# Cross-attention on one core: the first memory block loaded early, and a new order of transfers at the entry into the attention

## What is computed

```python
memory_proj = einsum('bme,de->bmd', memory, W_mem)
scores = einsum('bnd,bmd->bnm', hidden_states, memory_proj) / sqrt(D)
attn = softmax(scores)
memory_context = einsum('bnm,bmd->bnd', attn, memory_proj)
gate = sigmoid(concatenate([hidden_states, memory_context]) @ W_gate.T + b_gate)
fused = hidden_states + gate * memory_context
out = rmsnorm(fused) * norm_w
```

## Time and profile before

| | |
|---|---|
| median of 3 runs | 1613.51 us (1610.14 to 1613.7) |
| the profiled execution's own time | 1613.78 us |
| its span (first to last instruction) | 1612.0 us |
| mean granted TensorE clock | 0.995 of full |
| PE busy | 1578.6 us, 98% of the span |
| DVE busy | 1035.4 us, 64% |
| ACT busy | 458.2 us, 28% |
| DMA | mean 158 GB/s |

### The profile page before, as it was taken

One profiled execution on the slowest core, in us unless ns is written; L12 is line 12 of the kernel. 1 busy time (PEld: TensorE's weight loads), 2 busy tenths in 40 slices (PEclk: granted clock), 3 DMA queues, 4 the chain that ended last, 5 costly groups with the idle time before them and its releaser, 6 DMA issues.

```text
span 1612.0 us, 21593 instructions
## 1 busy us (share of the span) xinstructions
PE 1578.6 (98%) x6912; PEld 1302.4 (81%) x6912; DVE 1035.4 (64%) x1437; ACT 458.2 (28%) x767; POOL 17.9 (1%) x37
## 2 busy tenths in 40 slices
PE   7999999999999889999999999999999999999998
PEld 5888888888888768888888877887888888888886
DVE  5664668777777654576456744666545677777766
ACT  4333342222222332244223432253224211111111
POOL 0000000000000000000000000000000000000000
PEclk9999999999999999999999999999999999999999
DMA  9997533333334848566575748467555544444452
GB/s 200 237 225 172 137 105 118 104 116 114 113 118 122 190 125 200 146 173 178 157 176 143 201 145 198 132 166 186 152 177 148 177 164 168 169 173 158 169 182 98
DMA packets 211618, 255.22 MB, mean 158 GB/s; under 512 B 19840, under 2 KB 136576, under 8 KB 211328
## 3 DMA queue, kind: packets, MB, share of 16 engines
q1 hardware_dynamic: 211584, 254.87, 56.9%
HBM read 166.72 MB, written 85.98 MB: 157 GB/s over the span
## 4 chain that ended last, share of the span: by engine, by line
issue 99%; POOLq 0%; POOL 0%; DVE 0%; DVEq 0%
POOL rstd L585 0%; POOLq L583 0%; DVE region_f L1257 0%; POOLq L585 0%; DVEq L49 0%; POOL minus_half L581 0%; POOLq L1456 0%
## 5 line engine op out<-in xcount | busy, mean ns | idle before, releaser
L1283 PE MATMUL bank<-region_t,region_l 128*128 128x512 f32 x3072 | 704.5, 390 | 7.3 <-DVE region_l L266 5.2
L1283 PEld LDWEIGHTS bank<-region_t,region_l 128*128 128x128 f32 x3072 | 576.9, 188 | 130.3 <-issue 10.6
L1283 PE MATMUL bank<-region_n,region_l 128*128 128x512 f32 x1536 | 356.4, 391 | 5.9 <-DVE region_l L266 5.9
L1283 PEld LDWEIGHTS bank<-region_n,region_l 128*128 128x128 f32 x1536 | 290.3, 189 | 67.0 <-DVE region_l L266 6.4
L1283 PE MATMUL bank<-region_t,region_n 128*128 128x512 f32 x960 | 220.7, 392 | 10.8 <-DVE region_t L266 10.8
L1283 PEld LDWEIGHTS bank<-region_t,region_n 128*128 128x128 f32 x960 | 181.8, 190 | 49.2 <-DVE region_t L266 11.2
L723 ACT CAST region_l<-bank 128x512 fp32r<-128x512 f32 x128 | 75.0, 586 | 344.9 <-DVE bank L1066 344.7
L1066 DVE STREAM_TRANSPOSE bank<-region_f 128x512 f32<-128x512 f32 x128 | 88.7, 716 | 128.0 <-DMA region_f<-prob_scratch 125.8
L266 DVE TENSOR_TENSOR region_t<-region_f,region_t 128x1024 fp32r<-128x1024 f32 (+2 forms) x70 | 102.1, 1492 | 67.6 <-ACT region_t L597 60.5
L1324 PE MATMUL bank<-region_t,region_l 128*128 128x512 f32 x576 | 135.8, 389 | 0.0
L1324 PEld LDWEIGHTS bank<-region_t,region_l 128*128 128x128 f32 x576 | 108.1, 188 | 22.5
(11 more groups left out here) (58 smaller groups left out, 882.6 us busy)
## 6 DMA issues: line engine op xcount, KB each, us to landing
region_f<-in_ctx SPq DMA_DIRECT2D x128, 256.0 KB, 5.8
prob_scratch<-prob SPq DMA_DIRECT2D x128, 256.0 KB, 2.7
region_f<-prob_scratch SPq DMA_DIRECT2D x128, 256.0 KB, 4.5
region_f<-in_x SPq DMA_DIRECT2D x64, 256.0 KB, 6.1
region_f<-in_x SPq DMA_DIRECT2D x128, 128.0 KB, 2.7
region_f<-zx_scratch SPq DMA_DIRECT2D x32, 512.0 KB, 3.4
region_f<-in_x SPq DMA_DIRECT2D x32, 512.0 KB, 3.2
out<-region_f SPq DMA_DIRECT2D x31, 512.0 KB, 2.8
```

What stands on the lines that cost most here:

```text
L1283: mm = nc.tensor.matmul(dst, lhs(a), rhs(b), start=first and n == 0, stop=last and n == len(PASSES) - 1)
```

## The change

The raw mt block 0 gets tiles 8 and 9 and is loaded some 260 us earlier, right behind the loads of z pair 2. Its transposes go to tiles 0 and 1 (they were 8 and 9), one product earlier in pair 14. Blocks 1 to 3 are then loaded in the order of use, 1, 2, 3, where it was 3, 1, 2. Of the mn loads, block 1 comes as soon as mt halves 0 to 3 are split, block 0 still ahead of the exchange of unit 0, and block 2 goes behind that exchange, where only block 3 stood.

```diff
-        MT0_SLOT = (0, 1, 2, 0)
-        MT0_TF = [f_tile[k] for k in (8, 9, 8, 9, 2, 3, 4, 5)]
+        mt0_raw = [F[:, 4 * KW * k:4 * KW * (k + 2)] for k in (8, 2, 4, 8)]
+        mt0_tf = [f_tile[k] for k in (0, 1, 0, 1, 2, 3, 4, 5)]
...
+            sp.wait_ge(w7_ready, W7[S1])
+            load_mt(0, 0, mt0_raw[0])
+            with sp.Fori(0, NPAIR - 3) as p:
+                pair_sp(p)
+            pair_sp(NPAIR - 3, loads=False)
...
-            sp.wait_ge(zt_t, 2 * NPAIR)
-            load_mt(0, 0)
             p = NPAIR - 2
             store_zx(p, 0, slice(0, BANK), EV_C11, zx_stored[0])
-            sp.wait_ge(mt_t, HPJ)
-            load_mt(0, 3, MT0_SLOT[3])
-            store_zx(p, 1, slice(0, D), EV_C21, zx_stored[2])
             sp.wait_ge(z_ready, NPROD * NPAIR - 1)
             load_mt(0, 1)
-            store_zx(p, 0, slice(BANK, D), EV_C12, zx_stored[1])
+            store_zx(p, 1, slice(0, D), EV_C21, zx_stored[2])
             sp.wait_ge(z_ready, NPROD * NPAIR)
             load_mt(0, 2)
+            store_zx(p, 0, slice(BANK, D), EV_C12, zx_stored[1])
+            sp.wait_ge(mt_t, HPJ)
+            load_mt(0, 3, mt0_raw[3])
             store_zx(p + 1, 0, slice(0, BANK), EV_C11, zx_stored[0])
+            sp.wait_ge(mt_ready, HPJ * 2)
+            load_mn(0, 1)
             store_zx(p + 1, 1, slice(0, D), EV_C21, zx_stored[2])
+            store_zx(p + 1, 0, slice(BANK, D), EV_C12, zx_stored[1])
...
-            sp.wait_ge(mt_t, MTS)
-            load_mn(0, 1)
-            store_zx(p + 1, 0, slice(BANK, D), EV_C12, zx_stored[1])
-            sp.wait_ge(mt_ready, HPJ * 3)
-            load_mn(0, 2)
             for i in range(3):
                 sp.wait_ge(zx_stored[i], 16 * NPAIR)
             load_mn(0, 0)
             exchange(0, first=True)
+            sp.wait_ge(mt_ready, HPJ * 3)
+            load_mn(0, 2)
             sp.wait_ge(mt_ready, MTS)
             load_mn(0, 3)
...
-                if first and j == 1:
+                if first and j == 0:
+                    dve.wait_ge(zt_t, 2 * NPAIR)
+                elif first and j == 1:
                     dve.wait_ge(mt_ready, h - 1)
...
             def block_first(i):
+                if i == 2:
+                    mt_transpose(0, 0, first=True)
                 if i == 3:
-                    mt_transpose(0, 0, first=True)
-                if i == 4:
                     mt_transpose(0, 1, first=True)
```

More of the change, by code:

```diff
@@ L261, in tf_half @@
         def tf_half(h, first=False):
-            return (MT0_TF if first else b_tf)[h].rearrange("p (t m) -> p t m", t=CT)
+            return (mt0_tf if first else b_tf)[h].rearrange("p (t m) -> p t m", t=CT)
         def minus_hi(dst, src, hi):
@@ L392, in _, with load_mt @@
             load_zraw(2, 1)
[L393 to L398, removed]
+            def load_mt(b, j, dst=None):
+                load_quadrants(sp, b_in[j] if dst is None else dst, mem[b, BANK * j:BANK * (j + 1), :], C, mt_loaded[j])
             def load_mn(b, j):
@@ L1012, in mt_transpose @@
                     dve.wait_ge(mt_t, b * MTS + j * HPJ)
-                rows = b_in[MT0_SLOT[j] if first else j].rearrange("p (b t j) -> p t b j", t=CT, j=SQ)
+                rows = (mt0_raw if first else b_in)[j].rearrange("p (b t j) -> p t b j", t=CT, j=SQ)
                 nb = BANK // SQ // HPJ
```

## The result

| | before | changed |
|---|---|---|
| median of 9 runs | 1613.52 us (1610.14 to 1616.2) | 1608.92 us (1604.82 to 1610.09) |
| profiled span | 1612.0 us | 1607.1 us |
| ratio, 95% interval | | 0.9971 (0.9962 to 0.9979) |

The changed kernel is 4.6 us faster, 0.29%. Forecast were 1607.3 us (1603.5 to 1611.0) and a gain of 6.4 us. The sign is right and the time lies in the range; the median is 1.6 us above the forecast, and the shortfall lies in the second part, as the experiments show. By the prediction's own yardstick, that 4.8 us tell a change from none, these 4.6 us count as "same", which it gave 0.25; the interval of the ratio lies clear of 1 all the same.

What follows compares the result with a forecast made beforehand. PE, 98% busy, bounds the kernel; its entry loses 16.6 us to gaps and slow clock. Scores of unit 2 come 7.2 us earlier (3.9 from mt loads), minus 0.8 slow clock: 6.4 us off, 1607.3 us, range 1603.5 to 1611.0.

Steps and rivals of the forecast that it cites:

- second part: Exchange of unit 0 and mn loads at the entry: transposes 8.1 us earlier, scores of unit 2 at 578.5, not 585.74.
- First part: mt loads: block 1 first removes PE's gap at 527.96 and its slow stretch, 2.17 + 1.7 = 3.9 us.
- The early load costs nothing: Load of mt block 0 at about 241: no cost; without cover at most 4.5 us, once.
- Block 3 last of the mt loads: VectorE's transpose 6: block 3 lands by 534.5, needed at 534.8, 1.7 us slack; 2 us later costs 0.5 to 1.
- The exchange, 561.2: Unit 0's first transposes: first store 549.1 plus 11.0 exchange, 0.3 tail of mn 0, 0.85 for loads behind.
- The chain of 16.4 us: VectorE and ScalarE, transposes to scores of unit 2: not shortened, 16.4 us, so scores at 577.6 at the earliest.
- The landing of mn 3: Last mn load behind the exchange: lands at 568.7, between 566.9 and 570.4; scores of unit 2 9.8 us later.
- Slow clock in the scores of unit 2: PE's scores of unit 2 after small gaps: price 0 or 1.7 us, taken as 0.8.
- B: Second part gives its gain back: mn 3 at 571 or exchange at 564, plus slow clock; gain 3.2, 1610.5; chance 0.20.
- A: mn loads in time, queue behind the exchange costs nothing: scores of unit 2 at 576.5, gain 9.2, 1604.5; chance 0.15.
- Rival C: Loads behind the exchange mix with its last transfer, landing with mn 3 at 569: 1.4 us slower, 1615.2; chance 0.04.
- Rival D: mt block 1 still late, beyond 526; gap at 528 stays in part; gain 3 at most, 1610.8; chance 0.04.

Runs made afterwards that it cites:

- e10: The changed kernel, unaltered, measured and profiled once more: 1609.54 us, ratio 0.9965 against the kernel before.
- e1: Changed kernel with the mt part alone; mn loads and last z store as in the kernel before: 1610.05 us, ratio 0.9974.
- e3: Changed kernel with mt block 0 loaded late again and its transposes at their old places in pair 14: 1609.55 us, ratio 0.9978.
- e4: Changed kernel loading only the first 128 of 512 columns of mn blocks 2 and 3 of batch 0: 1605.73 us, ratio 0.995.
- e7: Changed kernel with mn 2 loaded ahead of mn 0 and so ahead of the exchange: 1607.9 us, ratio 0.9966.
- e5: Changed kernel with mn 3's cast and low part behind the last probability group, low part also behind unit 1's maxima: 1607.44 us, ratio 0.9958.
- e6: Changed kernel with the casts and low parts of mn 2 and mn 3 both moved behind the last probability group: 1606.81 us, ratio 0.996.

## Why the prediction was right, and where it was off

From the scores of unit 0, in us:

| | before | forecast | changed | changed again (e10) |
|---|---|---|---|---|
| first store of probabilities | 13.0 | 13.0 | 13.0 | 13.0 |
| first transposes | 29.3 | 25.1 | 25.7 | 24.5 |
| cast of mn 3 | 33.9 | 32.6 | 34.9 | 34.0 |
| scores of unit 2 (D) | 45.7 | 42.4 | 44.7 | 43.8 |

- **First part, 3.9 us: right.** The gap and its slow stretch are gone, and e1 alone gains 4.2 us by the ratio, 3.9 by the medians. "The early load costs nothing" holds; that it gives a microsecond at most (e3) was not said.
- **Block 3 last of the mt loads: right, with more air than said.** Transpose 6 doesn't wait in the changed kernel; in e3 it does, 0.53 us, and PE takes no harm.
- **The exchange, 561.2: nearly right.** 25.7 and 24.5 us from the scores of unit 0, forecast 25.1. Its tail of 0.85 us "for loads behind" was 1.6 in one profile and 0.4 in the other (end of issues to transposes: 5.3 and 4.1 us against 3.65). That the sum came out is in part luck: this stretch alone scatters by 2.6 us, from 3.3 to 5.9, over the profiles with 2 MB behind it.
- **The chain of 16.4 us, and 9.8 us from mn 3's landing to the scores: exact.** 16.4 in e1, e4 and e7; 9.8 in the changed kernel (571.64 to 581.43) and in e10 (570.55 to 580.34).
- **The landing of mn 3: the term that was mis-sized.** Forecast 568.7 (566.9 to 570.4), which is 32.6 us after the scores of unit 0; measured 34.9 and 34.0. From the first issue the two blocks took 14.4 us in the first profile and 13.6 in the second: at the forecast's upper bound, and beyond it. The rate for the second block was right: it landed 4.5 us after the first in both (567.17 to 571.64, 566.07 to 570.55), as that bound has it. Wrong was the lower bound, 1.8 us of start and 8.3 of data from the issue on, and the middle taken because of it. When SP issued the first block, the exchange's own transfers still stood ahead of it in the queue, and these landed only with the transposes, 5.3 and 4.1 us later. So the landings are better counted from the transposes: the first block 4.7 and 5.1 us behind them, the second 4.5 behind the first, 9.2 and 9.5 us in all. The forecast left 568.7 - 561.2 = 7.5 us for this, its lower bound 5.7, which would be 280 and 370 GB/s for 2.1 MB, above the 253 it worked with. The row for it was there: before, mn 3 alone was cast 573.93 - 569.31 = 4.6 us after the transposes, which makes 9.2 for two. With it the sum is 25.1 + 9.2 + 9.8 = 44.1 us of D, and the measured parts add up: 25.7 + 9.2 + 9.8 = 44.7 and 24.5 + 9.5 + 9.8 = 43.8.
- **Slow clock in the scores of unit 2, 0.8 us: did not come.** They took 11.17 us, and 11.04 to 11.19 in every run. This paid back part of the above.

So the forecast of the gain in D, 45.7 - 42.4 = 3.3 us, was 1.0 and 1.9 in the two profiles, and with the 3.9 us of the first part the entry yields 4.9 to 5.8 us. The span fell by 4.9 us. In that profile PE was 0.8 us behind at the last z pairs, by a later start (first matmul at 10.47 us where it was 9.46), and lost 1.0 us less in small gaps after unit 2 (4.2 in place of 5.2 us).

Rivals: B is close to what happened. Its scores of unit 2 at 580.8 are a D of 44.7 us, and its first reason (mn 3 at 571) came true in the first profile; its slow clock did not happen. A fails at its landing of mn 3 by 566.7. Rival C is out: the exchange's last transfer landed 4.7 and 5.1 us ahead of the first block behind it, not with the second. Rival D is out: block 1 came in time. For A's loads the prediction named the 341 GB/s for 1 MB of the Trainium skill, "DMA: Bandwidth & Descriptors", section "Bandwidth"; the page has them for a transfer onto 128 partitions that GpSimd issues, and these are four loads of 256 KB onto 32 partitions each, issued by SyncE. A block each 4.5 us is 235 GB/s, and the measurement decides. Against C the prediction also had, from the section "Queues, rings and completion order" of that page of the Trainium skill, that by ring order "even the 0.85 would be 0". That goes beyond the section, which has descriptors taken in ring order but lets a later one finish its write first; the traces have 0.4 and 1.6 us there.

A slip that changes nothing: the most to gain is 16.6 - 3.8 = 12.8 us, not 12.9.

Why the mn part brings so little is shown by e4, e5 and e7 from three sides: less data behind the exchange, mn 3 out of the softmax chain, or one block moved into idle time of the DMA ahead of the exchange each give back 1.8 to 3.5 us of D against the first profile, 0.9 to 2.6 against the second. In the time only e4 stands nearly clear of the changed kernel (3.2 us by the medians); for e5 and e7 the time alone would not show it. The idle time that e7 uses is smaller than its expectation says: in the changed kernel's trace the DMA moves nothing from 541 to 542 and next to nothing from 543 to 544, with a z store between.

## What to carry to other kernels

A transfer that is moved behind an urgent one only changes places with it: look for the latest of the two, and for what is queued on each engine behind its wait. Here the exchange came 3.6 to 4.8 us sooner, and the last block, no sooner than before, held back a softmax that didn't need it, because its cast stood ahead of the softmax's in the program. A load is best moved to where the DMA is idle, and its consumer behind everything that doesn't need it. And to price a load that is issued behind a transfer in the same queue, count from the landing of that transfer, not from the issue: here each 1 MB block landed 4.2 to 5.3 us after what stood ahead of it, in every profile in which ScalarE waited for it.

## What was unexpected of the hardware

The same gap is followed by a slow clock in one execution and not in the next. The gap of 2.06 to 2.07 us ahead of the scores of unit 1 was followed by 12.7 to 12.8 us for 48 matmuls in eight profiles and by 11.2 in five (e3, e5, e6, e7, e10). In the changed kernel it was followed by a stretch at 0.50 and the later gaps of 2.40, 1.94, 1.40 and 1.38 us by none:

```profile
551.00:553.00 2.00, 2.00 (x6) 1.52 (x6) 0.32 (x2) 2.00 (x4) 0.00 (x0) 0.50 0.96 320
...
563.00:575.00 12.00, 8.06 (x34) 6.38 (x35) 9.55 (x14) 5.95 (x6) 0.00 (x0) 1.00 0.65 138
```

In e10, the same program, it was the other way round: 1.00 after the gap of 2.06 us, and 7.08 us for the 24 matmuls after a gap of 2.71. So near 2 us a gap alone doesn't tell what clock follows, in this kernel worth 1.6 us for the 48 matmuls behind the gap of 2.06. What does tell is not shown.
